# Attention: the fourth score of the next step behind the weighted sum on TensorE

## The chip, the cores and the metric

The kernel runs on one core of a Trainium2 chip. The metric is the device time of one execution in microseconds (us); before the change three executions gave 3975.45, 3980.73 and 3981.07 us, a median of 3980.73 us.

## The reference

A transformer layer on 8 sequences of 2048 tokens with 256 channels. Attention has 16 heads of 16 channels; keys and values come from a strided convolution and so have 1024 rows per sequence:

```python
q = x @ q_w.T + q_b
xd = conv1d(x, conv_w, stride=2, groups=C) + conv_b
k = xd @ k_w.T + k_b
v = xd @ v_w.T + v_b
att = softmax(einsum('bhnd,bhmd->bhnm', q, k) / sqrt(D))
out = einsum('bhnm,bhmd->bhnd', att, v)
x = layernorm(x + out @ out_w.T + out_b)
```

Behind it stands a feed-forward part with a hidden width of 1024 (layernorm, dequantized weights, silu), a residual and a last layernorm.

## The kernel before

The program has four stages, one behind the other: `setup` (weights), `project` (q, k, v to DRAM), `attention` and `finish` (output projection and feed-forward). Only `attention` is touched.

**Tiling.** Attention handles 32 blocks of 512 queries. A block has 32 steps: 4 groups of 4 heads, and in each group 8 steps of 128 keys. So there are 1024 steps. What a step computes:

- *Four scores* (`score`, L590, matmul L602), u = 0 to 3, one per head: 128 keys by 512 queries. Heads 0 and 2 use rows 0 to 48 of the array, heads 1 and 3 use rows 64 to 112, so two of different parity can run side by side. Each score fills one bank of a ring of three PSUM banks, `score_ps` (`bank`, L496).
- *Four exponentials* (`exps`, L652, L658) on ScalarE, one per score, into `probs`, which has two buffers. One group ends with a copy of the result, `o_sb` (L668), on the same engine.
- *The weighted sum* (`weigh`, L605, L612): eight matmul instructions (four heads, two passes each in the profile) that add probs times v into `pv_ps`.
- *Four "first" matmuls* (`first`, L566, L577) for a step 12 steps ahead (LEAD): queries by keys, two into `first_ps0` and two into `first_ps1`. VectorE reduces each pair to a row maximum (`maxima`, L683), which later enters the scores as an extra row.
- Once a group, at step 4 of its 8 (TURN = 4), a *transpose of the maxima* (`turn_max`, L582, L588) that takes a turn in the ring of banks; VectorE copies it (`rows`, L697), and the queue of SyncE writes it into `q_s` (L512).

**Order on TensorE.** TensorE works through a list written out by hand (`one_block`, L616). For step s it is: scores 0 and 1 of step s+1, firsts 0 and 1, score 2 of step s+1, firsts 2 and 3, score 3 of step s+1, weighted sum of step s, and the transpose where due. In the last 12 steps of the program there are no firsts left to do.

**Waits.** A score u of step k waits until the exponential that last read its bank is done. With a ring of three, that is the one three places back: score 3 of step k waits for exponential 0 of step k, score 0 for exponential 1 of step k-1, score 1 for exponential 2 of step k-1, score 2 for exponential 3 of step k-1:

```python
pe.wait_ge(exped, 4 * (STEPS * n + s) + u + 1 + near)      # L600; exped starts at 3
pe.wait_ge(exped, 4 * (STEPS * n + s + 1) + RING)          # L610, weigh: exponential 3 of step s
act.wait_ge(scored, 4 * k + u + 1)                         # L657
```

In step 6 of a group (AFTER) scores 0 and 1 wait for one exponential more (`near`), since the transpose took a bank, and score 2 also waits for the copied maxima (`row_up`, L598). Exponentials also wait for the weighted sum of two steps before (L655), the copy to `o_sb` for the last weighted sum of its group, and the first weighted sum of a group for that copy (L609). The queue of SyncE reloads `q_s` once all scores of a group are done (L524) and k and v once its weighted sums are done (L526).

Of the kernel before, what the change touches and what calls it, by code (L numbers as in the profile page):

```python
# [466 lines left out]
def attention(nc, e):  # L467
# [3 lines left out]
    with ctx:  # L471
# [24 lines left out]
        def bank(s, u):  # L496

            return score_ps[(4 * s + u + (s - AFTER + KT) // KT) % RING]
# [63 lines left out]
        @block.tensor  # L562
        def _(pe):
            def first(n, part, u):

                g, r = part // KT % G, part % KT  # L566
                n1 = n + part // STEPS
                keys, h = u // 2, u % 2
                if r == 0 and u == 0:
                    pe.wait_ge(q_loaded[g], QL * (n1 + 1))  # L570
                    if isinstance(n1, int) and n1 == 0:
                        pe.wait_ge(kv_loaded[g], KVL)
                t, a = r // 2, r % 2
                if h == 0:
                    pe.wait_ge(first_used, 2 * (STEPS * n + part) + keys + 1)
                at = slice(h * HALF, h * HALF + KROWS)
                done = pe.matmul(first_ps[keys][:, h, :], q_s[g][at, a, t * P:(t + 1) * P],  # L577
                                 k_s[g][at, a, keys * 512:(keys + 1) * 512], start=True, stop=True)
                if h == 1:
                    done.then_inc(first_mm, 1)  # L580

            def turn_max(n, s):  # L582

                g = (s - TURN) // KT + 1
                pe.wait_ge(maxed, G * n + g + 1)
                if s > 0:
                    pe.wait_ge(exped, 4 * (STEPS * n + s + 1) + 2 + RING)
                pe.transpose(bank(s + 1, 4)[0:TT * HG, 0:P], neg_max[g % 2][:, :], ident[:, :]).then_inc(turned, 1)  # L588

            def score(n, s, u, more):  # L590

                n, s = (n + 1, 0) if s == STEPS else (n, s)
                g, t, a, h = s // KT, s % KT, u // 2, u % 2
                if t == 0 and u == 0:
                    pe.wait_ge(m_loaded[g], 1 + ML * (n + 1))
                behind_turn = t == AFTER
                if behind_turn and u == 2 and (more or s + KT - 2 < STEPS):
                    pe.wait_ge(row_up, 1 + G * n + g + 2)  # L598
                near = behind_turn and u < 2
                pe.wait_ge(exped, 4 * (STEPS * n + s) + u + 1 + near)  # L600
                at = slice(h * HALF, h * HALF + KROWS + 1)
                pe.matmul(bank(s, u)[:, :], k_s[g][at, a, t * P:(t + 1) * P],  # L602
                          q_s[g][at, a, :], start=True, stop=True).then_inc(scored, 1)

            def weigh(n, s):  # L605

                g, t = s // KT, s % KT
                if t == 0:
                    pe.wait_ge(o_up, 1 + G * n + g)  # L609
                pe.wait_ge(exped, 4 * (STEPS * n + s + 1) + RING)  # L610
                for h in range(HG):
                    last = pe.matmul(pv_ps[h * VC:(h + 1) * VC, :], v_s[g][:, t, h, :], probs[s % 2][:, h, :],  # L612
                                     start=t == 0, stop=t == KT - 1)
                last.then_inc(pv_done, 1)

            def one_block(n, more):  # L616
                for s in range(STEPS):
                    ahead = more or s + LEAD < STEPS
                    follow = more or s + 1 < STEPS
                    if follow:  # L620
                        score(n, s + 1, 0, more)
                        score(n, s + 1, 1, more)
                    if ahead:
                        first(n, s + LEAD, 0)
                        first(n, s + LEAD, 1)
                    if follow:
                        score(n, s + 1, 2, more)
                    if ahead:
                        first(n, s + LEAD, 2)
                        first(n, s + LEAD, 3)  # L630
                    if follow:
                        score(n, s + 1, 3, more)
                    weigh(n, s)
                    if s % KT == TURN and (more or s + KT < STEPS):
                        turn_max(n, s)

            pe.sem_inc(first_used, 2)  # L637
            pe.sem_inc(exped, RING)
            for part in range(LEAD):
                for u in range(4):  # L640
                    first(0, part, u)
                if part - LEAD == TURN - KT:
                    turn_max(0, part - LEAD)
            for u in range(4):
                score(0, 0, u, True)
            with pe.Fori(0, NB - 1) as n:
                one_block(n, True)
            one_block(NB - 1, False)

        @block.scalar  # L650
# [437 lines left out]
```

## Time and profile before

| | |
|---|---|
| median of three runs | 3980.73 us |
| profiled execution | 3983.98 us, its span 3982.2 us |
| mean granted TensorE clock | 0.982 |
| PE busy (matmul) | 3858.0 us, 97% |
| VectorE busy | 3302.4 us, 83% |
| ScalarE busy | 2639.5 us, 66% |
| attention, first to last weighted sum | about 338 to 3056 us |
| finish | the rest, to 3982 us |

PE is the matmul part of TensorE, PEld its weight loads; DVE is VectorE, ACT ScalarE, POOL GpSimd, SPq the DMA queue of SyncE. A matmul waits for its semaphore on its weight load, so the row of the weight load shows when the wait ended. A matmul whose weights were loaded ahead starts without a load just before it. A row of the timeline gives the start, the time from the start to the end of what the row merges (x2, x4, x8 instructions), and in brackets the idle time of that engine before it with what ended it. Starts are rounded to 0.01 us.

### The profile page before, as it was taken

To read this page: it belongs to the slowest core of one execution; us is meant where nothing else is said; L and a number is where in the kernel's file an instruction comes from. 1 tells how busy PE (TensorE), PEld (TensorE's weight loads), DVE (VectorE), ACT (ScalarE), POOL (GpSimd) and SP (SyncE) were. 2 spreads that over 40 slices of the span, in tenths; PEclk is the share of its full clock that TensorE was granted. 3 is DMA by queue.
4 is the path that set the end of the run, shared out by engine and by line. 5 is a ranking of instruction groups with operands and counts; after the bars stand their busy time and mean duration, and the time that the engine had idled before them with its cause. 6 is when DMAs were issued, how large, how long until landed. Compare 5 with 4: busy or idle time off the path is not lost. (4 is left out here: it accounts for less than half of the span.)

```text
span 3982.2 us, 77196 instructions
## 1 busy us (share of the span) xinstructions
PE 3858.0 (97%) x22952; PEld 2013.6 (51%) x22952; DVE 3302.4 (83%) x4116; ACT 2639.5 (66%) x5028; POOL 818.9 (21%) x535
## 2 busy tenths in 40 slices
PE   7988999999999999999999999999997799999998
PEld 5663333333333333333333333333332689999998
DVE  5658999999999999999999999999993677778775
ACT  3445888888788788888888888887874333433343
POOL 5440000000000000000000000000000677877875
PEclk9997999999999999999999999999997899999999
DMA  7993114112211411311131141122111222222220
GB/s 247 337 329 66 34 33 83 30 33 56 57 33 33 81 33 33 66 47 33 44 70 33 33 82 31 33 55 58 33 38 51 72 73 76 84 79 69 84 83 28
DMA packets 217854, 286.13 MB, mean 72 GB/s; under 512 B 25521, under 2 KB 127921, under 8 KB 217778
## 3 DMA queue, kind: packets, MB, share of 16 engines
q1 hardware_dynamic: 217778, 285.33, 25.7%
q8 instruction: 22, 0.36, 0.0%
q14 instruction: 54, 0.44, 0.0%
HBM read 165.69 MB, written 118.49 MB: 71 GB/s over the span
## 5 line engine op out<-in xcount | busy, mean ns | idle before, releaser
L683 DVE TENSOR_REDUCE half_max<-first_ps 128x2 f32<-128x1024 f32 x2048 | 2413.3, 1221 | 263.3 <-PE first_ps L577 259.2
L658 ACT ACTIVATE probs<-score_ps 128x512 f32<-128x512 f32 x4096 | 2114.9, 603 | 569.5 <-PE score_ps L602 569.4
L602 PE MATMUL score_ps<-q_s,k_s 49*128 49x512 f32 x4096 | 1440.0, 476 | 21.8 <-DMA q_s<-max_row 7.3
L602 PEld LDWEIGHTS score_ps<-q_s,k_s 49*128 49x128 f32 x4096 | 571.7, 185 | 1285.2 <-ACT probs L658 1174.7
L612 PE MATMUL pv_ps<-probs,v_s 128*32 128x512 f32 x8192 | 1099.4, 609 | 0.0
L577 PE MATMUL first_ps<-k_s,q_s 48*128 48x512 f32 x4096 | 905.8, 422 | 20.9 <-PEq L637 12.8
L1042 POOL TENSOR_TENSOR num<-num,rden 128x1024 f32<-128x1024 f32 x32 | 83.8, 2619 | 2784.8 <-DMA rden<-rden_d 2784.8
L899 ACT ACTIVATE act_f<-fc_ps,b 128x512 f32<-128x512 f32 x256 | 175.4, 685 | 454.4 <-PE fc_ps L854 452.3
L577 PEld LDWEIGHTS first_ps<-k_s,q_s 48*128 48x128 f32 x4096 | 402.9, 187 | 73.6 <-DVE half_max L683 18.6
L975 DVE CAST a_hi<-act_f 128x512 fp32r<-128x512 f32 x256 | 251.8, 984 | 142.1 <-ACT act_f L899 141.8
L1023 POOL TENSOR_TENSOR a_lo<-act_f,a_hi 128x512 fp32r<-128x512 f32 x256 | 339.5, 1331 | 79.4 <-DVE a_hi L975 79.4
L867 PE MATMUL fc_ps<-w_hi,a_hi 128*128 128x256 f32 x1024 | 294.4, 287 | 0.9 <-DVE r L961 0.9
L612 PEld LDWEIGHTS pv_ps<-probs,v_s 128*32 128x32 f32 x8192 | 161.7, 108 | 252.1 <-ACT probs L658 149.4
L867 PE MATMUL fc_ps<-w_lo,a_hi 128*128 128x256 f32 x1024 | 286.1, 279 | 0.0
L867 PE MATMUL fc_ps<-w_hi,a_lo 128*128 128x256 f32 x1024 | 286.0, 279 | 0.0
L854 PE MATMUL fc_ps<-h_hi,w_hi 128*128 128x512 f32 x512 | 204.1, 399 | 8.5 <-ACT act_f L899 5.6
L854 PE MATMUL fc_ps<-h_lo,w_hi 128*128 128x512 f32 x512 | 203.5, 398 | 0.0
L854 PE MATMUL fc_ps<-h_hi,w_lo 128*128 128x512 f32 x512 | 203.2, 397 | 0.0
L867 PEld LDWEIGHTS fc_ps<-w_hi,a_hi 128*128 128x128 f32 x1024 | 192.3, 188 | 9.0 <-POOL a_lo L1023 1.2
L867 PEld LDWEIGHTS fc_ps<-w_lo,a_hi 128*128 128x128 f32 x1024 | 192.2, 188 | 7.4
L867 PEld LDWEIGHTS fc_ps<-w_hi,a_lo 128*128 128x128 f32 x1024 | 192.0, 188 | 0.0
L834 PE MATMUL proj_ps<-wo,num 128*128 128x256 f32 x512 | 118.8, 386 | 20.8 <-POOL num L1042 20.8
(83 smaller groups left out, 2427.8 us busy)
## 6 DMA issues: line engine op xcount, KB each, us to landing
q_s<-q_hi_d SPq DMA_DIRECT2D x512, 64.0 KB, 2.1
o_d<-o_sb SPq DMA_DIRECT2D x128, 256.0 KB, 2.1
x_in<-x_in SPq DMA_DIRECT2D x32, 512.0 KB, 5.2
q_hi_d<-q_hi SPq DMA_DIRECT2D x32, 512.0 KB, 3.4
q_lo_d<-q_lo SPq DMA_DIRECT2D x32, 512.0 KB, 4.2
v_d<-v_f SPq DMA_DIRECT2D x32, 512.0 KB, 4.5
k_s<-k_hi_d SPq DMA_DIRECT2D x128, 128.0 KB, 4.2
v_s<-v_d SPq DMA_DIRECT2D x32, 512.0 KB, 6.4
```

The source lines that it names most:

```text
L577: done = pe.matmul(first_ps[keys][:, h, :], q_s[g][at, a, t * P:(t + 1) * P], k_s[g][at, a, keys * 512:(keys + 1) * 512], start=True, stop ...
L602: pe.matmul(bank(s, u)[:, :], k_s[g][at, a, t * P:(t + 1) * P], q_s[g][at, a, :], start=True, stop=True).then_inc(scored, 1)
L612: last = pe.matmul(pv_ps[h * VC:(h + 1) * VC, :], v_s[g][:, t, h, :], probs[s % 2][:, h, :], start=t == 0, stop=t == KT - 1)
L658: nc.scalar.activation(probs[s % 2][:, u, :], bank(s, u)[:, :], ACT.Exp).then_inc(exped, 1)
L683: dve.reduce_max(half_max[g % 2][:, :, a * TT + t, keys], first_ps[keys][:, :, :], AX.X)\
L834: last = pe.matmul(proj_ps[t // 2][:, t % 2, :], num[j][:, c, t * P:(t + 1) * P], wo[:, c, :], start=c == 0, stop=c == CC - 1)
L854: last = pe.matmul(fc1_ps[f % 2][:, :], w[:, c, cut], h[:, c, :], start=i == 0, stop=i == len(pairs) - 1)
L867: last = pe.matmul(fc2_ps[t // 2][:, t % 2, :], a[j][:, f, cut], w[:, f, :], start=f == 0 and i == 0, stop=f == FC - 1 and i == 2)
L899: nc.scalar.activation(act_f[f % RING][:, :], fc1_ps[f % 2][:, :], ACT.Silu, bias=b1[:, f:f + 1]).then_inc(act_up, 1)
L975: dve.tensor_copy(a_hi[j][:, f, :], act_f[f % RING][:, :]).then_inc(ahi_up, 1)
L1023: pool.tensor_tensor(a_lo[j][:, f, :], act_f[f % RING][:, :], a_hi[j][:, f, :].bitcast(F32), ALU.subtract)\
L1042: pool.tensor_tensor(num[j][:, :, :], num[j][:, :, :], rden[j][:, :, :], ALU.mult).then_inc(attn_up, 1)
```

## The change

In the hand-written list of TensorE the fourth score of step s+1 (u = 3) changes places with the weighted sum of step s. No instruction is added or removed, no wait and no other engine's list is altered. The transpose, where due, stays behind both.

```diff
@@ -628,9 +628,9 @@
                     if ahead:
                         first(n, s + LEAD, 2)
                         first(n, s + LEAD, 3)
+                    weigh(n, s)
                     if follow:
                         score(n, s + 1, 3, more)
-                    weigh(n, s)
                     if s % KT == TURN and (more or s + KT < STEPS):
                         turn_max(n, s)
```

## Rows read from the trace of the kernel before

**Rows 1.** The profile's page: busy time, share of the span and instructions of each engine.
```profile
PE 3858.0 (97%) x22952; PEld 2013.6 (51%) x22952; DVE 3302.4 (83%) x4116; ACT 2639.5 (66%) x5028; POOL 818.9 (21%) x535
```

**Rows 2.** Waits from 1000 to 2000 us: who for whom, total us, times, longest.
```profile
PEld score_ps L602 <- ACT probs L658: 435.5, 709, 1.6
ACT probs L658 <- PE score_ps L602: 189.8, 331, 1.3
DVE half_max L683 <- PE first_ps L577: 88.9, 331, 1.1
```

**Rows 3.** Timeline of all engines, 1507.1 to 1509.8 us: one plain step.
```profile
1507.13 0.19 PEld L602 LDWEIGHTS score_ps<-q_s,k_s 49*128 49x128 f32 x2 [0.84 <-ACT probs L658]
1507.48 0.39 PE L577 MATMUL first_ps<-k_s,q_s 48*128 48x512 f32 x2
1507.67 2.07 ACT L658 ACTIVATE probs<-score_ps 128x512 f32<-128x512 f32 x4 [0.54 <-PE score_ps L602]
1507.71 0.40 PE L602 MATMUL score_ps<-q_s,k_s 49*128 49x512 f32 x1
1507.92 2.36 DVE L683 TENSOR_REDUCE half_max<-first_ps 128x2 f32<-128x1024 f32 x2 [0.25 <-PE first_ps L577]
1508.32 0.18 PEld L602 LDWEIGHTS score_ps<-q_s,k_s 49*128 49x128 f32 x1 [0.42 <-ACT probs L658]
1508.32 0.49 PE L602 MATMUL score_ps<-q_s,k_s 49*128 49x512 f32 x1
1508.74 0.16 PEld L612 LDWEIGHTS pv_ps<-probs,v_s 128*32 128x32 f32 x8 [0.24 <-issue]
1509.74 0.19 PEld L602 LDWEIGHTS score_ps<-q_s,k_s 49*128 49x128 f32 x2 [0.84 <-ACT probs L658]
```

**Rows 4.** ScalarE's timeline, 1507.6 to 1507.7 us: exponential 0 of that step alone.
```profile
1507.67 0.60 ACT L658 ACTIVATE probs<-score_ps 128x512 f32<-128x512 f32 x1 [0.54 <-PE score_ps L602]
```

**Rows 5.** Instructions of line 612 from 1000 to 2000 us: duration min/median/max.
```profile
L612 PEld LDWEIGHTS pv_ps<-probs,v_s x3024: 106/108/110, 999.9 to 1997.8; 128*32 128x32 f32 x189
```

**Rows 6.** Weight loads, 1510 to 1525 us: the transpose, then a score 2 held up.
```profile
1513.95 0.16 PEld L612 LDWEIGHTS pv_ps<-probs,v_s 128*32 128x32 f32 x8 [0.24 <-issue]
1514.94 0.09 PEld L588 LDWEIGHTS score_ps<-ident,neg_max 128*16 128x16 f32 x1 [0.84 <-ACT probs L658]
1515.15 0.19 PEld L602 LDWEIGHTS score_ps<-q_s,k_s 49*128 49x128 f32 x2
1515.72 0.18 PEld L602 LDWEIGHTS score_ps<-q_s,k_s 49*128 49x128 f32 x1 [0.27 <-DVE max_row L697]
1515.81 0.21 PEld L577 LDWEIGHTS first_ps<-k_s,q_s 48*128 48x128 f32 x2
1516.76 0.16 PEld L612 LDWEIGHTS pv_ps<-probs,v_s 128*32 128x32 f32 x8 [0.24 <-ACT probs L658]
```

**Rows 7.** PE's timeline, 1516.1 to 1516.4 us: the two firsts behind that score.
```profile
1515.81 0.63 PE L577 MATMUL first_ps<-k_s,q_s 48*128 48x512 f32 x2
```

**Rows 8.** Timeline, 1500 to 1510 us: two weighted sums around a group's end, and the copy.
```profile
1500.84 0.16 PEld L612 LDWEIGHTS pv_ps<-probs,v_s 128*32 128x32 f32 x8 [0.25 <-ACT probs L658]
1501.97 0.60 ACT L668 ACTIVATE o_sb<-pv_ps 128x512 f32<-128x512 f32 x1
1503.53 0.16 PEld L612 LDWEIGHTS pv_ps<-probs,v_s 128*32 128x32 f32 x8 [0.24 <-issue]
```

**Rows 9.** Stretches: us, busy (x count) of PE, PEld, DVE, ACT, POOL, clock, DMA.
```profile
3014.00:3024.00 10.00, 8.64 (x49) 2.49 (x48) 7.60 (x6) 7.38 (x15) 0.00 (x0) 1.00 0.00 1
3024.50:3040.00 15.50, 14.54 (x48) 3.87 (x48) 3.48 (x2) 8.18 (x16) 0.00 (x0) 0.50 0.05 18
400.00:3000.00 2600.00, 2589.26 (x15850) 1002.13 (x15842) 2362.18 (x2213) 2090.24 (x4055) 0.00 (x0) 1.00 0.19 46
```

**Rows 10.** Weight loads, 3009 to 3034 us: two weighted sums at the lower clock.
```profile
3029.27 0.20 PEld L612 LDWEIGHTS pv_ps<-probs,v_s 128*32 128x32 f32 x8 [0.44 <-issue]
3033.40 0.20 PEld L612 LDWEIGHTS pv_ps<-probs,v_s 128*32 128x32 f32 x8 [0.44 <-ACT probs L658]
```

## The prediction

> **What bounds the kernel now.** I read the page first. PE is busy 97% [rows 1], which tempts one to say that TensorE's work is the limit; but matmuls are pipelined, and a busy PE is not a full one. So next come the waits inside attention. In 1000 us the weight loads of scores stood waiting for exponentials for 435.5 us, ScalarE waited 189.8 us for scores, and VectorE 88.9 us for firsts [rows 2]. Each waits for another: no engine is full, and a loop through several sets the pace. The timeline of one plain step shows the loop [rows 3]:
>
> - scores 0 and 1 load at 1507.13; exponential 0 starts at 1507.67: 0.54 us;
> - it takes 0.60 us [rows 4], and score 3 of the same step loads at 1508.32, 0.05 after its end: 0.65 us. That load stood 0.42 us waiting for it;
> - the weighted sum of the step before loads at 1508.74: 0.42 us behind score 3. It had all its inputs long ago, since score 2 waits for the same exponential; it stands only behind score 3 in TensorE's list;
> - scores 0 and 1 of the next step load at 1509.74: 1.00 us for the weighted sum.
>
> 0.54 + 0.65 + 0.42 + 1.00 = 2.61 us, the whole step. A group of eight steps has six such steps or their like, one with the transpose (1513.95 to 1516.76, 2.81 us [rows 6]) and one over its end (1500.84 to 1503.53, 2.69 us [rows 8]). 6 x 2.61 + 2.81 + 2.69 = 21.16 us; from 1000 to 2000 us there are 3024 / 8 = 378 weighted sums [rows 5], so 2.646 us each and 21.16 us in eight. The reading closes.
>
> **What the change removes.** Score 3 is no longer between exponential 0 and the weighted sum. The weighted sum starts as soon as firsts 2 and 3 are through, and the 0.42 us wait and the 0.42 us of score 3 leave this loop. By itself that is a gain. Score 3, issued behind the 1.00 us of the weighted sum, finds exponential 0 long done and waits for nothing.
>
> **What it makes late.** Exponential 3 of a step needs score 3, which now comes 1.00 us later. And score 2 of the next step, the weighted sum and hence the next score 3 all stand behind exponential 3. So there is a second loop, once a step:
>
> - exponential 3, then the wake of score 2's load: 0.60 + 0.05 = 0.65 us, the same two instructions as in the old loop [rows 3, 4];
> - from that load through score 2 and firsts 2 and 3 to the load of the weighted sum: x;
> - the weighted sum, to the load of score 3: 1.00 us [rows 3];
> - score 3 to the start of exponential 3: 0.54 us, as from score 0 to exponential 0 [rows 3].
>
> The period is 2.19 + x. The old one is 2.19 + 0.42. So the whole change, in a plain step, is x against 0.42 us: the stretch in front of the weighted sum held one score and will hold a score and two firsts.
>
> **The size of x.** In the plain step score 2 is not late, so its row does not give x. But behind the transpose it was late for another reason: its load woke at 1515.72 [rows 6], and the two firsts behind it ended at 1515.81 + 0.63 = 1516.44 [rows 7], 0.72 us later. How long before the recorded end of a matmul may the weighted sum load? Score 3 ended at 1508.32 + 0.49 = 1508.81, the weighted sum loaded at 1508.74 [rows 3], 0.07 before. So x = 0.72 - 0.07 = 0.65 us. From below it is bounded by 0.42 (a lone score; the firsts would have to cost nothing), from above by 0.84 (score and the first on the same rows one behind the other, each 0.42 with its load exposed). I take 0.65, since its row is this very sequence, and 0.60 to 0.70 for its error. The period is then 2.84 us, 0.23 more than 2.61.
>
> The Trainium skill bears on x. In the late case the loads of firsts 2 and 3 began at 1515.81, within the 0.18 us load of score 2 and well before its matmul ended [rows 6], and first 2 uses the same rows of the array. "TensorE: Matmul & The Clock Gate", Part 3, "The mechanism", states that weight loads overlap matmuls in flight only where the row group differs, though it also grants loads into a background buffer; by the strict half of it x would be 0.84 us. The row decides for the other half.
>
> **Does another limit come first?** At 2.84 us per step, VectorE needs 2.36 [rows 3], ScalarE 2.07 (2.67 where it copies `o_sb`). TensorE, after score 3, can run ahead: score 0 beside score 3, score 1 beside first 0, first 1; 0.58 us on the rows of scores and firsts (1507.13 to 1507.71 [rows 3]). Score 3's load to the next score 2's wake is 0.54 + 0.65 = 1.19 us. So TensorE stands idle for some 0.6 us in front of score 2, and it hides scores 0, 1 and firsts 0, 1 at no cost; that cover is why they don't appear in the loop. Score 3 has no DMA; reloads of q now wait for a score that ends later, 12 steps ahead of their use: free.
>
> **Special steps.** The transpose cost 0.21 us (1514.94 to 1515.15 [rows 6]) on the old path; now it stands in the idle time behind score 3: minus 0.21. But two steps after it a score 1 needs exponential 3 in place of exponential 2 (`near`), so score 1 with first 0 also stands in the loop, one more wave of 0.23 us (1507.48 to 1507.71 [rows 3]): plus 0.23. At a group's end the 0.60 us copy stands between exponential 3 and the next exponential 0 [rows 8], which was on the old loop and cost 2.69 - 2.61 = 0.08. In the new one it runs beside score 2, and the weighted sum, 0.65 + 0.65 behind the start of exponential 3, finds it done (exponentials start (2.07 - 0.60) / 3 = 0.49 apart, so 0.49 + 0.60 + 0.05 = 1.14): minus 0.08.
>
> **The sum.** A group: 8 x 0.23 + 0.23 - 0.21 - 0.08 = 1.78 us. The last 12 of 1024 steps have no firsts, x is again 0.42 and they lose nothing. (1024 - 12) / 8 = 126.5 groups x 1.78 = 225 us. The other stages are untouched. The profiled execution took 3983.98 us with a span of 3982.2; it would take 4209. The median lies 3 us lower, so I predict 4206 us, 5.7% slower. With x of 0.60 a group loses 1.38 us (4155), with 0.70 it loses 2.18 (4257).
>
> **The rivals.**
>
> *A. Faster: the second loop does not close.* If exponential 3 is always over when score 2 comes up, both loops are gone and VectorE is next, with 2.36 us of reductions a step [rows 3]: (2.61 - 2.36) x 1012 = 253 us less, 3728 us. The place is the wait of score 2 for exponential 3; it decides for a gain once x is under 0.42. For it: today that wait is met, as score 2's matmul follows the firsts at 1507.71 with no gap. Against: today score 3 comes 1.0 us earlier. The code's own count of the wait names exponential 3. 3%.
>
> *B. No change: firsts 2 and 3 hide beside score 2.* Then x is 0.42, and only the group's end is won: 8 us, about 3973. Against: the late case took 0.72. 3%.
>
> *C. Slower by more: x = 0.84.* 8 x 0.42 - 0.06 = 3.30 us a group, 4398 us. Against: the loads at 1515.81. 3%.
>
> *D. The clock.* From 400 to 3000 us the granted clock is 1.00 (2.4 GHz). The firsts ended at about 3014 us; the clock was still 1.00 from there to 3024 and was 0.50 (1.2 GHz) behind it [rows 9], with 4.13 us from one weighted sum to the next [rows 10]. The new step has the old matmuls in more time, and more idle time in front of score 2. Were the clock halved all through, a step, which has four firsts more than those, would take at least 4.13 us: + 1.52 x 1012 = 1540 us, 5520 us. Against: the old loop kept its clock with 0.42 us of idle loads a step, and through waits of up to 1.6 us [rows 2]. 4%; a fall for a part of the time would land between.
>
> *The forecast*: slower by x = 0.65, 87%.
>
> **The numbers.** A measurement of this kernel can tell about 0.2%, 8 us, from no change. Faster: A, 3%. Same: B, 3%. Slower: the rest, 94%. The range takes in x from 0.60 to 0.70 and an unplanned 15 us above: 4150 to 4275; outside lie A, B, C and D, 13%, and a small part of the forecast's own case.
>
> **What the profile should show.** Weight loads of the weighted sum 2.84 us apart. The load of score 3 directly behind the weighted sum, waiting for nothing, and scores 0 and 1 close behind it. The idle loads in front of score 2, ended by ScalarE, some 0.6 us. ScalarE idle for 0.7 us or more before exponential 3, no longer before exponential 0. VectorE idle for 0.48 us a step in place of 0.25. Group ends without the copy's 0.08. I am wrong if score 2 waits for nothing, if the stretch from its load to the weighted sum is not 0.65, or if the granted clock leaves 1.00 before the firsts end.

## The result and the profile after

The changed kernel takes 4219.06 us (median of four, 4210.19 to 4228.93) against 3980.9 us: ratio 1.060, 95% interval 1.057 to 1.063. The forecast was 4206 us, 4150 to 4275. The profiled execution took 4228.93 us with a span of 4227.1, 244.9 us longer than the span before.

The first part of the profile's page: TensorE has the same instructions and is busy for a smaller share of the span; VectorE's and ScalarE's busy times are nearly unchanged ([rows 1] before).
```profile
PE 3925.4 (93%) x22952; PEld 1966.3 (47%) x22952; DVE 3302.8 (78%) x4116; ACT 2659.5 (63%) x5028; POOL 818.9 (19%) x535
```

The waits from 1000 to 2000 us, to be laid beside [rows 2]. The three rows of that group have grown, and all of it is waiting, not work. The fourth row here names ScalarE, but score 2 waits for the same exponential: it is the time in which score 2 and firsts 2 and 3 pass in front of the weighted sum:
```profile
PEld score_ps L602 <- ACT probs L658: 503.4, 694, 0.8
ACT probs L658 <- PE score_ps L602: 254.2, 347, 0.9
DVE half_max L683 <- PE first_ps L577: 155.7, 304, 0.9
PEld pv_ps L612 <- ACT probs L658: 110.5, 303, 0.4
```

The timeline of one plain step, 1502.6 to 1505.5 us, answers to [rows 3]:
```profile
1502.63 0.30 PEld L602 LDWEIGHTS score_ps<-q_s,k_s 49*128 49x128 f32 x3 [0.84 <-ACT probs L658]
1502.74 0.42 PEld L577 LDWEIGHTS first_ps<-k_s,q_s 48*128 48x128 f32 x2
1503.17 2.06 ACT L658 ACTIVATE probs<-score_ps 128x512 f32<-128x512 f32 x4 [0.78 <-PE score_ps L602]
1503.64 2.36 DVE L683 TENSOR_REDUCE half_max<-first_ps 128x2 f32<-128x1024 f32 x2 [0.43 <-PE first_ps L577]
1503.82 0.18 PEld L602 LDWEIGHTS score_ps<-q_s,k_s 49*128 49x128 f32 x1 [0.66 <-ACT probs L658]
1503.91 0.20 PEld L577 LDWEIGHTS first_ps<-k_s,q_s 48*128 48x128 f32 x2
1504.48 0.16 PEld L612 LDWEIGHTS pv_ps<-probs,v_s 128*32 128x32 f32 x8 [0.36 <-ACT probs L658]
1505.47 0.19 PEld L602 LDWEIGHTS score_ps<-q_s,k_s 49*128 49x128 f32 x2 [0.84 <-ACT probs L658]
```
This is the second loop. Score 3 loads at 1502.63, with scores 0 and 1 of the next step directly behind it (x3). Exponential 3 starts at 1503.17, 0.54 later, after ScalarE stood idle for 0.78 us; that idle time used to be in front of exponential 0. Score 2 wakes at 1503.82, 0.65 later, its load idle for 0.66 us before. The weighted sum loads at 1504.48: x is 0.66 us. The next score 3 loads at 1505.47, 0.99 later. Together 2.84 us. (The bracket of that load names an exponential, but the one that score 3 needs, exponential 0 of its step, is the one behind exponential 3 in the row of 1503.17, at some 0.60 us each, and so over by 1504.4; what passes in the 0.99 us is the weighted sum.)

Over all steps of the trace, by the median time from one weighted sum to the next at each place in a group, the seven plain steps take 2.83 to 2.85 us and the one behind the transpose 3.17; before, it was 2.60 to 2.61, with 2.81 at the transpose and 2.70 at the group's end. A block of four groups takes 92.27 us in place of 84.60.

The weight loads behind a transpose, 1510 to 1514.4 us, answer to [rows 6]:
```profile
1510.16 0.16 PEld L612 LDWEIGHTS pv_ps<-probs,v_s 128*32 128x32 f32 x8 [0.37 <-ACT probs L658]
1511.15 0.18 PEld L602 LDWEIGHTS score_ps<-q_s,k_s 49*128 49x128 f32 x1 [0.84 <-ACT probs L658]
1511.58 0.09 PEld L588 LDWEIGHTS score_ps<-ident,neg_max 128*16 128x16 f32 x1 [0.25 <-issue]
1512.34 0.18 PEld L602 LDWEIGHTS score_ps<-q_s,k_s 49*128 49x128 f32 x1 [0.37 <-ACT probs L658]
1512.44 0.20 PEld L577 LDWEIGHTS first_ps<-k_s,q_s 48*128 48x128 f32 x2
1512.64 0.18 PEld L602 LDWEIGHTS score_ps<-q_s,k_s 49*128 49x128 f32 x1
1513.33 0.16 PEld L612 LDWEIGHTS pv_ps<-probs,v_s 128*32 128x32 f32 x8 [0.36 <-ACT probs L658]
```
From the weighted sum to score 3 (1511.15) it is 0.99 us, from there to the wake of score 1 (1512.34) 1.19, which is 0.54 and 0.65 as in a plain step: the transpose between them adds nothing. From that wake to the weighted sum it is 0.99 us, 0.33 more than x.

### The profile page after: what moved, and what is told of

The parts are those of the page before. It is cut to its first block and busy times, and to the rows that moved or that the text cites. A ratio compares the mean times of both kernels' runs of the same rounds, so it can differ in the third digit from the quotient of the medians.

```text
span 4227.1 us, 77196 instructions
## 1 busy us (share of the span) xinstructions
PE 3925.4 (93%) x22952; PEld 1966.3 (47%) x22952; DVE 3302.8 (78%) x4116; ACT 2659.5 (63%) x5028; POOL 818.9 (19%) x535
## 5 line engine op out<-in xcount | busy, mean ns | idle before, releaser
L658 ACT ACTIVATE probs<-score_ps 128x512 f32<-128x512 f32 x4096 | 2150.4, 603 | 814.5 <-PE score_ps L602 809.7
L602 PE MATMUL score_ps<-q_s,k_s 49*128 49x512 f32 x4096 | 1350.5, 476 | 197.7 <-ACT probs L658 175.6
L577 PE MATMUL first_ps<-k_s,q_s 48*128 48x512 f32 x4096 | 1272.8, 428 | 20.3 <-PEq L637 12.2
L602 PEld LDWEIGHTS score_ps<-q_s,k_s 49*128 49x128 f32 x4096 | 534.2, 185 | 1534.4 <-ACT probs L658 1479.4
L577 PEld LDWEIGHTS first_ps<-k_s,q_s 48*128 48x128 f32 x4096 | 550.9, 187 | 65.8 <-DVE half_max L683 18.3
```

Source lines behind the costliest of these rows:

```text
L658: nc.scalar.activation(probs[s % 2][:, u, :], bank(s, u)[:, :], ACT.Exp).then_inc(exped, 1)
```

## The experiments

They are numbered in the order in which they were run and told by the question that they answer. In all of them the hand-written list of TensorE is walked by a loop over a tuple, so that an order can be named by step t of the group; "weigh" is the weighted sum. The changed kernel would read

```python
def order(t):
    return (("score", 0), ("score", 1), ("first", 0), ("first", 1), ("score", 2),
            ("first", 2), ("first", 3), ("weigh", 0), ("score", 3), ("turn", 0))
```

The first four ask whether the stretch x, and not the new place of score 3, is what costs.

**1. Firsts 2 and 3 behind score 3.**
```diff
-            ("first", 2), ("first", 3), ("weigh", 0), ("score", 3), ("turn", 0))
+            ("weigh", 0), ("score", 3), ("turn", 0), ("first", 2), ("first", 3))
```
and on VectorE, so that the copy of the maxima does not stand behind a reduction that now comes late (`maxima` takes the halves to be reduced as a third argument; that part is left out here):
```diff
-                    if more or s + LEAD < STEPS:
-                        maxima(n, s + LEAD)
-                    if s % KT == TURN and (more or s + KT < STEPS):
-                        rows(n, s)
+                    turning = s % KT == TURN and (more or s + KT < STEPS)
+                    for keys in half_rows:
+                        if more or s + LEAD < STEPS:
+                            maxima(n, s + LEAD, (keys,))
+                        if turning and keys == 0:
+                            rows(n, s)
```

> The order of the change, but firsts 2 and 3 behind score 3 (and, so that the copied maxima are not late, the copy in front of the second reduction on VectorE). The loop theory: the stretch from score 2's load to the weighted sum is a lone score again, 0.42 us, so the plain step falls from 2.84 to 2.61 us though score 3 keeps its new place; only the step two behind the transpose keeps its extra 0.33 us. A group of eight is 8 x 2.61 + 0.33 = 21.2 us against 21.15 before: about 3990 us, between 3975 and 4010. The rival, by which the new place of score 3 itself costs (its lone load behind the weighted sum, a drain more): the plain step stays at 2.8 us or more, 4200 us.

Measured: 3979.96 us against 3978.18, ratio 1.0007 (0.9998 to 1.0017). The timeline, 1520.6 to 1523.35 us (lines of this file are shifted by four or so):
```profile
1521.68 0.18 PEld L602 LDWEIGHTS score_ps<-q_s,k_s 49*128 49x128 f32 x1 [0.84 <-ACT probs L654]
1522.22 1.57 ACT L654 ACTIVATE probs<-score_ps 128x512 f32<-128x512 f32 x3 [0.54 <-PE score_ps L602]
1522.87 0.18 PEld L602 LDWEIGHTS score_ps<-q_s,k_s 49*128 49x128 f32 x1 [0.42 <-ACT probs L654]
1523.30 0.16 PEld L612 LDWEIGHTS pv_ps<-probs,v_s 128*32 128x32 f32 x8 [0.25 <-ACT probs L654]
```
Score 3 (1521.68) is still behind the weighted sum and exponential 3 still sets the pace, but x is 0.43 us (1522.87 to 1523.30) and the plain step 2.60. The whole cost is gone with two firsts out of the stretch. The rival falls. The edit on VectorE has no part in the plain step: experiment 9, without it, has plain steps of 2.60 to 2.61 too.

The time itself is nearer to the kernel before than the steps are. By its steps this order is still a little slower, as expected: its step behind the transpose takes 2.93 us, and a block 84.89 us against 84.60, 9 us in thirty blocks. In the profiled executions the last block gives that back, 81.0 us from its first weighted sum to its last against 93.0. At its end the granted clock was still 1.00 in this experiment; in the kernel before it was 0.50 over the last 31 us of attention.

**2. Four firsts between score 2 and the weighted sum.**
```diff
-    return (("score", 0), ("score", 1), ("first", 0), ("first", 1), ("score", 2),
+    return (("score", 0), ("score", 1), ("score", 2), ("first", 0), ("first", 1),
```

> The order of the change, but all four firsts stand between score 2 and the weighted sum. The loop theory: one wave of two firsts more in the stretch, 0.23 us, so it takes 0.89 us and the plain step 3.08 us. Scores 1 and 2 now start side by side, so the step behind the transpose pays nothing extra: 8 x 3.08 = 24.6 us a group, 3.5 us more than before, about 4425 us (4380 to 4450). The rival (score 3's place costs, firsts are hidden): unchanged from the changed kernel, 4219 us.

Measured: 4465.04 us, ratio 1.124 (1.120 to 1.128). The timeline, 1511 to 1515 us:
```profile
1512.53 0.18 PEld L602 LDWEIGHTS score_ps<-q_s,k_s 49*128 49x128 f32 x1 [0.88 <-ACT probs L654]
1512.63 0.42 PEld L577 LDWEIGHTS first_ps<-k_s,q_s 48*128 48x128 f32 x4
1513.41 0.16 PEld L612 LDWEIGHTS pv_ps<-probs,v_s 128*32 128x32 f32 x8 [0.36 <-issue]
```
x is 0.88 us and the median plain step 3.07 to 3.08, as expected. So x is 0.43, 0.66, 0.88 with none, two, four firsts: 0.22 to 0.23 us for each two. The sum is 40 us over the expected one, outside the stated 4380 to 4450: the step behind the transpose took 3.37 us, 0.30 more than a plain one, where none was expected (38 us over 126.5 groups). The trace shows what it waited for, 1530.3 to 1532.2 us:
```profile
1530.93 0.27 DVE L693 CAST max_row<-score_ps 16x128 fp32r<-16x128 f32 x1
1530.96 0.48 PEld L602 LDWEIGHTS score_ps<-q_s,k_s 49*128 49x128 f32 x2 [0.37 <-ACT probs L654]
```
Score 1 loads at 1530.96 and score 2 0.30 later (0.48 less its own 0.18). The copy of the maxima, which score 2 needs, ends at 1531.20, 0.06 before that load; it stood behind a reduction that comes late in this order. So here the 0.30 us are the late copy. In the changed kernel, where the same step is 0.33 us too long, the copy is over before scores 1 and 2 load; experiments 4 and 8 look at that.

**3. The same firsts moved in the kernel before.**
```diff
-    return (("score", 0), ("score", 1), ("first", 0), ("first", 1), ("score", 2),
-            ("first", 2), ("first", 3), ("weigh", 0), ("score", 3), ("turn", 0))
+    return (("score", 0), ("score", 1), ("first", 0), ("first", 1), ("first", 2),
+            ("first", 3), ("score", 2), ("score", 3), ("weigh", 0), ("turn", 0))
```

> The order of the kernel before, but firsts 2 and 3 in front of score 2. The loop theory: the old loop runs score 0, exponential 0, score 3, weighted sum; firsts and score 2 lie in the idle time in front of score 3, so nothing changes: 3981 us within 15. The rival, by which any first that moves in front of a score is paid: 0.23 us a step, 4215 us.

Measured: 3978.54 us, ratio 0.9997 (0.9987 to 1.0007). In its waits from 1000 to 2000 us the firsts now stand waiting for VectorE as long as VectorE stands waiting for them, and it costs nothing:
```profile
PEld score_ps L602 <- ACT probs L654: 407.9, 709, 1.5
PEld first_ps L577 <- DVE half_max L679: 90.2, 329, 0.4
DVE half_max L679 <- PE first_ps L577: 88.7, 329, 1.0
```
In the old loop no first stands between exponential 0 and the weighted sum that is not covered by score 3's wait. So a first costs nothing where it is covered by a wait, and costs time where it stands in the loop.

**6. The change in every other step.**
```diff
+    if t % 2:
+        return (("score", 0), ("score", 1), ("first", 0), ("first", 1), ("score", 2),
+                ("first", 2), ("first", 3), ("score", 3), ("weigh", 0), ("turn", 0))
```

> The change in every other step only (steps 0, 2, 4, 6 of a group). If the cost were a price on each moved score, half of it would remain: about 4100 us. The loop theory: in two steps the path goes score 3, exponential 3, exponential 0 of the next step, score 3 of that step, weighted sum, then scores 0 and 1, firsts, score 2, firsts, weighted sum: 0.54 + 0.49 + 0.65 + 0.42 + 1.00 + 1.14 + 1.00 = 5.24 us, 2.62 a step, as the kernel before, with steps of unequal length; the step behind the transpose pays some 0.3 more. A group is about 21.3 to 21.5 us: 4000 to 4030 us.

Measured: 4006.45 us, ratio 1.0063 (1.0045 to 1.0081). The weight loads, 1500 to 1508 us:
```profile
1501.91 0.16 PEld L612 LDWEIGHTS pv_ps<-probs,v_s 128*32 128x32 f32 x8 [0.24 <-issue]
1504.05 0.16 PEld L612 LDWEIGHTS pv_ps<-probs,v_s 128*32 128x32 f32 x8 [0.38 <-ACT probs L656]
1507.14 0.16 PEld L612 LDWEIGHTS pv_ps<-probs,v_s 128*32 128x32 f32 x8 [0.24 <-issue]
```
Steps of 2.14 and 3.09 us, 5.23 in two against the expected 5.24, and against 5.21 in the kernel before. Half the moves cost 27 us of 238, not half of it: the new loop is paid when it closes in every step, and here it closes only over two. The 27 us stand behind the transpose, where by the medians one step takes 3.31 us in place of 3.09 and the next 2.48 in place of 2.13.

The next two ask what the 0.33 us in the step behind the transpose are.

**4. Firsts 0 and 1 in front of score 1 in that step, in the changed order.**
```diff
+    if t == AFTER - 1:
+        return (("score", 0), ("first", 0), ("first", 1), ("score", 1), ("score", 2),
+                ("first", 2), ("first", 3), ("weigh", 0), ("score", 3), ("turn", 0))
```

> The changed kernel, but in the one step of eight in which scores 0 and 1 wait for one exponential more, firsts 0 and 1 stand in front of score 1, which then starts side by side with score 2. The loop theory: the 0.33 us that this step has over the plain one go, the rest stays: 126.5 x 0.33 = 42 us less than the changed kernel, 4177 us (4160 to 4190). The rival, by which the 0.33 us are the transpose itself or the wait for the copied maxima: no change, 4219 us.

Measured: 4193.67 us (4188.47 to 4214.29), 25 less than the changed kernel, where 42 less was expected. The step is 3.01 us long, so half of the 0.33 is gone, not all.

**8. As 4, and the wait for the copied maxima on score 1.**
```diff
-                if behind_turn and u == 2 and (more or s + KT - 2 < STEPS):
+                if behind_turn and u == 1 and (more or s + KT - 2 < STEPS):
                     pe.wait_ge(row_up, 1 + G * n + g + 2)
```

> The fourth experiment (the changed order with its special step mended), with the wait for the copied maxima on score 1. The theory of the two waits: another 0.16 us of a group go, 20 us, 4173 us (4160 to 4185), and the special step is as long as a plain one, 2.84 us. The rival: as the fourth experiment, 4194 us.

Measured: 4178.69 us (4162.88 to 4194.67), ratio 1.052 (1.049 to 1.054), and the step is 2.83 us, as long as the plain ones. The loads of scores 1 and 2 and of the weighted sum in 4 (1516.8 to 1519 us) and, below it, in 8 (1506.2 to 1508.3 us):
```profile
1518.00 0.35 PEld L602 LDWEIGHTS score_ps<-q_s,k_s 49*128 49x128 f32 x2 [0.25 <-ACT probs L656]
1518.83 0.16 PEld L612 LDWEIGHTS pv_ps<-probs,v_s 128*32 128x32 f32 x8 [0.34 <-ACT probs L656]
```
```profile
1507.41 0.19 PEld L602 LDWEIGHTS score_ps<-q_s,k_s 49*128 49x128 f32 x2 [0.25 <-ACT probs L656]
1507.52 0.19 PEld L577 LDWEIGHTS first_ps<-k_s,q_s 48*128 48x128 f32 x2
1508.07 0.16 PEld L612 LDWEIGHTS pv_ps<-probs,v_s 128*32 128x32 f32 x8 [0.36 <-ACT probs L656]
```
In 4 the two loads take 0.35 us: score 2 has two waits in front of it and loads 0.17 behind score 1, though the copy that the second one is for was over before score 1 loaded (by 0.16 us, the median over the groups). In 8 both load together (0.19), and 0.66 us later comes the weighted sum. The trace also shows an instruction for the second wait. Line 600 leaves these on the queue of TensorE, in 4 and, below it, in 8:
```profile
L600 PEldq EVENT_SEMAPHORE  x131: 51/51/51, 325.5 to 3239.7; - x131
L600 PEldq EVENT_SEMAPHORE  x7: 51/51/51, 324.6 to 3215.2; - x7
```
One a group is gone in 8. In 4 it stands at 1518.1 us, between the two loads. That going through it is what takes the 0.17 us is the likeliest reading. So of the 0.33 us a wave of firsts behind score 1 was 0.16 and the second wait 0.17, taken out in this order.

The last four start from experiment 1: two look for an order that beats both kernels, and two try its two edits one without the other.

**5. Experiment 1 with the order of 4 in the step behind the transpose.**
```diff
+    if t == AFTER - 1:
+        return (("score", 0), ("first", 0), ("first", 1), ("score", 1), ("score", 2),
+                ("weigh", 0), ("score", 3), ("turn", 0), ("first", 2), ("first", 3))
```

> The first experiment with firsts 2 and 3 behind score 3, and, in the one step of eight behind the transpose, firsts 0 and 1 in front of score 1. Its plain step stays 2.60 us; its special step was 0.33 us longer. The theory that score 2's second wait, for the copied maxima, is looked at only after its first: about half of the 0.33 goes, as in the fourth experiment, 20 us: 3960 us. The rival, that the fourth experiment's rest came from something in the changed order alone: all 0.33 go, 3938 us, or none, 3980 us.

Measured: 3957.93 us against 3979.26, ratio 0.9952 (0.9939 to 0.9966). Its special step (the one behind the transpose) is 2.77 us, its group's end 2.67. It is 0.5% faster than the kernel before and 6% faster than the changed one. By its steps about half of that 0.5% is earned: a block takes 84.29 us against 84.60, some 9 us in all. In the profiled executions the last block makes 12 us more (80.9 against 93.0), again with the clock at 1.00 to its end; what the clock does there was not tried.

**7. As 5, with the edit of 8.**

> The fifth experiment, with the wait for the copied maxima moved from score 2 to score 1 of that step, which itself comes late, so both loads wake on the same exponential. The theory of the two waits one behind the other: the remaining 0.15 us go, a group is 8 x 2.605 + 0.06 at its end = 20.9 us against 21.15 before, 126.5 x 0.25 = 32 us faster than the kernel before: about 3948 us (3940 to 3960). The rival, that the rest is the two late scores themselves: as the fifth experiment, 3960 us.

Measured: 3962.21 us, ratio 0.9957 (0.9942 to 0.9972): the same as 5 within the intervals, and not the expected 3948. The special step went from 2.77 to 2.75 us only. In this order the firsts 2 and 3 of the step before stand behind the transpose too, and in the trace a first of the next pair begins its matmul 0.03 us behind score 1's load, and the matmul of score 2 follows it 0.23 later. The rest is this queue of firsts, by the trace; it was not tried by itself.

**9. Experiment 1 without its edit on VectorE.**

> The first experiment without its edit on VectorE: the copy of the maxima stands again behind both reductions of its step. Firsts 2 and 3 of that step now issue behind score 3 and the transpose, their reduction ends over 2 us later, and the copy, score 2 behind it and the weighted sum wait for it. Plain steps stay 2.60 us; the step behind the transpose takes about 4.1 us in place of 2.93, 1.2 us a group, 150 us: about 4130 us (4100 to 4150). Were the edit on VectorE without effect: 3980 us.

Measured: 4199.52 us (two executions, 4177.15 and 4221.9), 70 over the expected value. The special step is 4.07 us, as expected. What was not expected is the clock. Stretches of this run (us, busy of PE, PEld, DVE, ACT, POOL, clock, DMA):
```profile
1519.50:1522.30 2.80, 2.06 (x12) 0.93 (x15) 2.37 (x4) 1.84 (x4) 0.00 (x0) 1.00 0.00 0
1522.40:1525.60 3.20, 3.20 (x16) 1.45 (x8) 0.98 (x2) 1.46 (x4) 0.00 (x0) 0.50 0.01 3
340.00:3270.00 2930.00, 2836.22 (x16345) 1085.90 (x16337) 2439.07 (x2278) 2185.51 (x4188) 0.00 (x0) 0.95 0.17 41
```
and weight loads around it:
```profile
1521.57 0.18 PEld L602 LDWEIGHTS score_ps<-q_s,k_s 49*128 49x128 f32 x1 [1.17 <-DVE max_row L693]
1522.00 0.16 PEld L612 LDWEIGHTS pv_ps<-probs,v_s 128*32 128x32 f32 x8 [0.24 <-issue]
1525.80 0.16 PEld L612 LDWEIGHTS pv_ps<-probs,v_s 128*32 128x32 f32 x8 [0.42 <-ACT probs L654]
1528.41 0.16 PEld L612 LDWEIGHTS pv_ps<-probs,v_s 128*32 128x32 f32 x8 [0.25 <-ACT probs L654]
```
Behind the 1.17 us wait for the copied maxima the granted clock fell to 0.50 (1.2 GHz), and the next step took 3.80 us in place of 2.60. This happened behind some of the transposes, not all; from 340 to 3270 us the mean clock was 0.95, where the kernel before and the changed one had 1.00 once it had risen, until the firsts had ended. An estimate from these rows: a mean of 0.95 is a tenth of the 2930 us at 0.50, and at 3.80 us in place of 2.60 for a step that costs about 90 us, as much as the profiled execution (4221.9) lies over the expected 4130.

**10. The kernel before with the edit on VectorE alone.**

> The kernel before with the edit on VectorE alone, to tell what of the fastest variant's gain it could carry. With the transpose behind the weighted sum, the second reduction of its step would wait for the transpose, and firsts for that reduction: the step behind the transpose grows by 0.5 to 0.9 us, a group by as much, 65 to 110 us: 4045 to 4090 us. Were the edit a gain by itself: below 3970 us.

Measured: 4055.86 us (two executions, 4055.4 and 4056.33), ratio 1.020 (1.012 to 1.028); the special step is 3.45 us in place of 2.81. The edit on VectorE is a loss alone, and experiment 1 needs it: an order on VectorE fits one order on TensorE.

## Why the prediction was right

**The old loop** was read rightly: experiment 3 moved firsts within it at no cost, and it closes on 2.61 us.

**The new loop** was read rightly, term by term: 0.54, 0.65, 0.66 and 0.99 us measured for 0.54, 0.65, 0.65 and 1.00. The row of the late score 2 [rows 6, 7] gave x within 0.01 us. Experiments 1 and 2 changed x, and the plain step followed: 2.60, 2.84 and 3.08 us with none, two and four firsts in the stretch. The firsts load at 1503.91, inside the load of score 2 (1503.82, 0.18 long) and before its matmul has ended. The Trainium skill, "TensorE: Matmul & The Clock Gate", Part 3, "The mechanism", lets weight loads overlap matmuls in flight only where the row group differs, and it lets the queue pull a load ahead into the background weight buffer as well. The trace agrees with the second and not with the first: with the first x would have been 0.84 us, and it was 0.66.

**The cover** held: scores 0 and 1 and firsts 0 and 1 have loaded by 1503.16, and TensorE's loads then stand idle for 0.66 us in front of score 2. **The group's end** held: the median step there is 2.85, as the plain ones. **The transpose** itself went off the path.

**The one term that was mis-sized** is the step behind the transpose. The prediction put "one more wave of 0.23 us"; it is 0.33. The wave was there, but it was worth 0.16 when experiment 4 took it out, and score 2's second wait, which the prediction did not count, stands in the loop as well, with the 0.17 that experiment 8 took out. That the sum was off by 0.10 only is in part luck: one part was too large and the other missing. A group lost 92.27 / 4 - 84.60 / 4 = 1.92 us and not 1.78. Of the 0.14 us between them 0.10 stand in that step, and the rest is hundredths in the others. In all that makes 243 us and not 225.

**The rest** of the 244.9 us is small. The first steps of attention run before the clock has risen, and the prediction left them out. At 0.50 the new step takes 4.49 us. The stretches of the changed kernel:
```profile
336.00:360.00 24.00, 24.00 (x91) 8.17 (x89) 13.27 (x14) 10.78 (x21) 0.00 (x0) 0.50 0.00 1
362.00:3270.00 2908.00, 2719.43 (x16256) 980.27 (x16256) 2423.43 (x2266) 2165.91 (x4163) 0.00 (x0) 1.00 0.18 42
```
The first block took 101.6 us, 9.3 over a later one; before it was 86.0, 1.4 over: plus 8 us. The last 12 steps, without firsts, took 2 us less than before; at either clock they are as long as before or a little shorter (4.07 us against 4.13 at 0.50), but the clock fell 24 us before their end and not 31. The other 20 steps of the last block lost 1 us less (they had been 2.67 us long), 1 us of waits for reloads was gone, and the stages around attention took 1 us less. The four executions fall in two pairs, 4210 and 4212 us at mean clocks of 0.988 and 0.987, 4226 and 4229 at 0.982. That the difference lies in when the clock rises and falls is likely, but only the profiled one, of the second pair, was seen in its stretches, and it was not tried. The profiled execution of experiment 4, at a mean clock of 0.987, speaks for it: there the clock was 1.00 from 338 to 3262 us, the first block took 1 us over a later one and not 9, and the last 12 steps took 31 us and not 40.

**The rivals.** A (faster) and B (no change) both needed x at or under 0.42; experiment 1, with x = 0.43, gives 3980 us where B said 3973, so the point from which the change is a loss was right. C (x = 0.84) did not come. D (the clock) did not come in the changed kernel: its clock stayed at 1.00 from 362 to 3270 us in spite of 0.66 us idle loads. But experiment 9 shows that it was a real risk: with one 1.17 us wait a group the clock fell behind some of them. Its price was right as a lower bound: the prediction said at least 4.13 us a step at 0.50, and the new step took 4.49.

## What to carry to other kernels

When an instruction is moved off a critical loop (a ring of waits through several engines that sets the time of a step), write down the loop that its own consumers close, with everything that stands between in the queue, before counting the gain: here a loop of 2.61 us was opened and one of 2.84 closed, and the difference was two matmuls that had cost nothing where they stood. Look in the old trace for a place where the same sequence already runs late; its rows size the new stretch better than the rows of the covered case. And a cost found in a loop is not a price per move: half the moves cost a ninth. Last, the total of this kernel also holds 10 to 20 us that go with when the clock rises and falls at the ends of attention; the step times tell two orders apart better.

## What was not expected of the hardware

- A weight load with a second wait in front of it came 0.17 us behind its neighbour that woke on the same event (0.35 against 0.19 us for the two loads, experiments 4 and 8), though what the second wait was for had been done before. The trace of 4 has one more instruction a group for it on TensorE's queue.
- With a single idle load of 1.17 us a group the granted clock fell from 1.00 to 0.50 behind some of them (experiment 9), while with idle loads of 0.66 us in each of 1000 steps it stayed at 1.00 (the changed kernel). The fall cost 1.2 us in the step shown (3.80 against 2.60).
- At a clock of 0.50 each pair of firsts in the loop costs about twice as much. The first steps of attention, all at 0.50, take 4.07 us with no first in the stretch (experiment 7), 4.49 with two (the changed kernel) and 4.91 with four (experiment 2): 0.42 us for each two, against 0.22 to 0.23 at 1.00.
